# A graph and expert network on one core: counting sums spread over all eight groups, expert zero's first tile started earlier, and low parts placed ahead of two neighbours

## The chip, the core and the metric

The kernel runs on one core of a Trainium2 chip. The metric is the device time of one launch in microseconds. TensorE (PE) does the matrix products, VectorE (DVE) and ScalarE (ACT) the element work, GpSimd (POOL) index work and indirect transfers, SyncE (SP) issues most of the transfers.

## What is computed

3125 rows of 256 numbers pass four residual blocks; the graph has 50000 edges in both directions and a loop at each node (103125 entries, sorted by target). Cut to what matters:

```
def conv(h, Wl, bl, Wr):                       # mean over a node's neighbours
    agg = segment_sum(h[src], dst); mean = agg / max(count, 1)
    return mean @ Wl.T + bl + h @ Wr.T
def gnn(h, ...):  return conv(relu(conv(h, W1...)), W2...)

x = x + gnn(layernorm(x), L0_gnn)              # first network
n = layernorm(x)                               # 8 experts, top 2, without gate weights
x = x + sum over the two best e of (gelu(n @ W1[e] + b1[e]) @ W2[e] + b2[e])
x = x + gnn(layernorm(x), L1_gnn)              # second network, same graph
n = layernorm(x)                               # 4 small experts, top 2, and a shared one
x = x + shared(n) + gated(n)
```

## The kernel before, in words

The rows are padded to 25 tiles of 128. A convolution's sum over neighbours is a dense product with the adjacency matrix of counts, which stays in on-chip memory as f16 (`adj`); the rows are split into a high and a low f16 part (`parts`). Every engine has a program of its own, written out in order and tied to the others by semaphores. The stages follow one another:

1. `first_block` (0 to 80 us): layer norm, the first dense products, the edge keys. `Normalise.vector_norm` (line 295) computes mean and root for a chunk of five tiles (CT) and scales them with `norm_apply` (187); after one semaphore `transpose_chunk` (203 to 207) turns them on PE. `sync` stores the products `zt` (lines 662 to 681).
2. `build_counts` (80 to 320 us, from line 1056): 88 groups of windows of the sorted edges, in 11 bodies (BODIES) of 8 groups (UNROLL). For a group DVE makes two one-hot selections (563), PE multiplies them in 12 matmuls (`count`, 1261), and ACT copies the counts into `adj` (1208). There are two slots (SLOT): DVE can select for group g when PE has counted g-2. PE then adds up the neighbours of the 288 targets of the body before (`add_up`, 1272; 100 matmuls over 25 tiles into two banks), and ACT empties the banks (`take_sums`, 1191) into memory. The 25 tiles are shared out over the groups: four or five behind each of the counts 1 to 6 of a body, none behind 7 and 0. The first body only counts. A rare case (a window with more edges than fit) has a program of its own behind `flag`, which each engine reads before the first body.
3. `second_conv` of the first network (320 to 560 us): a ring of neighbour sums is loaded and scaled on DVE (`neighbours`, 1383 and 1385), rectified on ACT (`relu`, 1388), multiplied by the two weights on PE (1925), and the product split into its high part on ACT (`high`, 1865) and its low part on DVE (`take`, 1713). As parts come, PE sums early output tiles (1949), later ones in `one_tile` (1964). At its end come layer norm and gate, a rank and a place for each row and choice (`choose`, `put`), in seven groups of tiles of SIZES (4, 4, 4, 4, 4, 3, 2), and POOL scatters the rows to their experts' slots (`slots_in`, CAP rows for each expert). `Route` (2078 to 2158) then builds tables with the tile count, first tile and slot address; SP and ACT clear the 256 slots behind each expert's last row (`clear`, 2109 to 2121, four transfers each, and the tail of `x1`).
4. `experts` (582 to 812 us, 2162 to 2340): 28 tiles of 256 rows (ST) over the 8 experts. SP loads a tile (2205), PE turns it (2230), ACT copies it, PE does the first product (2237), ACT gelu (2292), PE the second product (2247), which is issued behind the turn of the next tile. DVE adds the bias into the one output buffer `y` (2306) when the adds of the tile before have landed, POOL copies the ids (2323) and issues two indirect transfers that add the rows to `x1` (2328).
5. `weigh_and_sum` (812 to 1013 us): layer norm of the second network in chunks, its first convolution over the finished `adj`.
6. `second_conv` again, for the second network (1013 to 1232 us, without routing), and `last_experts` (to 1382 us).

The change touches `count` and `add_up`'s order on PE and what answers it on DVE and ACT, the order in front of `take(0)` in `second_conv`, `Route`, `experts`, `Normalise`, and `first_block`'s stores.

## Time and profile before

| | us |
|---|---|
| median of 3 runs | 1375.41 (1374.94 to 1382.29) |
| the profiled execution | 1383.73 |
| its span | 1382.3 |
| PE busy | 1233.4 (89%) |
| PE weight load busy | 919.0 (66%) |
| DVE busy | 576.0 (42%) |
| ACT busy | 400.6 (29%) |
| POOL busy | 163.8 (12%) |

The profile is of one execution, whose time is 8.3 us above the median; durations in the trace are from that one. Its page gives each engine's busy time and the busy share in 40 slices; the table of stretches gives the same for stretches of one's own choice, with the clock granted to PE (1.00 is 2.4 GHz, 0.50 is 1.2 GHz). In the timeline a row is a run of like instructions: start, length, engine, line, what is written from what, how many, and in square brackets the engine's idle time just before and what ended it. `PEld` is the load of weights beside PE, `SPq` the queue of SP, where transfers are issued.

### The profile page before, as it was taken

How to read it: one execution, taken by the hardware profiler on the slowest of the kernel's cores; microseconds unless marked ns; L12 is line 12 of the kernel's file. 1: busy time of each engine (PE TensorE's matmuls, PEld its weight loads, DVE VectorE, ACT ScalarE, POOL GpSimd, SP SyncE). 2: the span in 40 equal slices, each digit the busy share in tenths (PEclk: the TensorE clock that was granted, in tenths of full speed). 3: DMA queues.
4: the chain of work that ended last, by engine and by line, in shares of the span. 5: the costliest groups of instructions: out<-in, count | busy, mean ns of one | idle time of the engine just before them, and what ended most of it. 6: DMA issues, size and time to landing. Idle time of an engine off the chain costs nothing. (4 is left out here: it accounts for less than half of the span.)

```text
span 1382.3 us, 22037 instructions
## 1 busy us (share of the span) xinstructions
PE 1233.4 (89%) x7906; PEld 919.0 (66%) x7906; DVE 576.0 (42%) x1495; ACT 400.6 (29%) x798; POOL 163.8 (12%) x177
## 2 busy tenths in 40 slices
PE   5969999998999987199999949999979999989998
PEld 4648778775668665088888837655546677866675
DVE  7857777753445545300101026200024444256444
ACT  3543443431221001164446513300012211123322
POOL 4000000000000424334344410000000000000000
PEclk9989999999999989599999979999999999989999
DMA  6200000015652323535664542120046533135001
GB/s 195 74 22 10 17 11 15 17 32 132 174 137 85 100 81 96 174 57 102 138 130 76 99 93 83 57 64 28 27 101 166 152 125 120 65 91 169 19 19 36
DMA packets 133067, 117.03 MB, mean 85 GB/s; under 512 B 22691, under 2 KB 121380, under 8 KB 132993
## 3 DMA queue, kind: packets, MB, share of 16 engines
q1 hardware_dynamic: 100896, 74.71, 19.0%
q0 software_dynamic: 11984, 18.77, 7.1%
q10 hardware_dynamic: 20112, 22.56, 4.9%
q8 instruction: 48, 0.79, 0.3%
q14 instruction: 27, 0.21, 0.1%
HBM read 67.01 MB, written 48.99 MB: 84 GB/s over the span
## 5 line engine op out<-in xcount | busy, mean ns | idle before, releaser
L1272 PE MATMUL b_pa<-adj,l_parts 128*128 (+1 forms) x1100 | 145.6, 287 | 1.9 <-ACT ring L1191 1.9
L1208 ACT ACTIVATE adj<-b_pw 128x450 f32 (+1 forms) x176 | 87.1, 550 | 136.9 <-PE b_pw L1261 136.9
L1272 PEld LDWEIGHTS b_pa<-adj,l_parts 128*128 128x128 f16 x1100 | 106.1, 98 | 26.7 <-ACT adj L1208 2.0
L563 DVE TENSOR_TENSOR ring<-it,key 128x1800 f16<-128x1800 f16 x88 | 96.3, 1094 | 55.6 <-PE b_pw L1261 54.3
L1261 PE MATMUL b_pw<-ring,room 128*128 128x150 f16 x1056 | 86.7, 234 | 25.4 <-DVE room L563 18.4
L2306 DVE TENSOR_TENSOR ring<-l_sum,l_parts 128x512 f32<-128x512 f32 x28 | 19.4, 692 | 215.0 <-DMA x<-ring,l_ids_now 114.8
L2247 PE MATMUL l_sum<-l_parts,ring 128*128 128x256 f32 x448 | 104.2, 385 | 4.1 <-ACT ring L2292 0.6
L1964 PE MATMUL l_sum<-l_parts,adj 128*128 128x256 f16 x750 | 95.0, 286 | 10.6 <-issue 10.6
L1261 PEld LDWEIGHTS b_pw<-ring,room 128*128 128x128 f16 x1056 | 76.8, 100 | 32.0 <-DVE room L563 22.0
L2247 PEld LDWEIGHTS l_sum<-l_parts,ring 128*128 128x128 f32 x448 | 82.8, 190 | 21.0 <-ACT ring L2292 10.9
L1964 PEld LDWEIGHTS l_sum<-l_parts,adj 128*128 128x128 f16 x750 | 75.0, 102 | 30.8 <-issue 19.5
L2328 POOL DMA_INDIRECT x<-ring,l_ids_now x56 | 86.6, 1546 | 56.2 <-DVE ring L2306 47.6
L1383 DVE SCALAR_TENSOR_TENSOR ring<-ring,unscale 128x256 f32<-128x256 f32 x50 | 23.9, 477 | 160.0 <-DMA ring<-inv 160.0
L1964 PE MATMUL l1b_sum<-l_parts,adj 128*128 128x256 f16 x750 | 84.8, 273 | 0.0
L563 DVE TENSOR_TENSOR room<-ib,low 128x1536 f16<-128x1536 f16 x88 | 83.7, 951 | 0.0
L1964 PEld LDWEIGHTS l1b_sum<-l_parts,adj 128*128 128x128 f16 x750 | 72.6, 98 | 12.6 <-issue 4.3
L2530 ACT ACTIVATE l_parts<-m_bank,adj 128x320 f32<-128x320 f32 x90 | 47.0, 528 | 80.2 <-PE m_bank L2477 53.6
L1949 PEld LDWEIGHTS l1b_sum<-l_parts,adj 128*128 128x128 f16 x500 | 49.8, 100 | 24.6 <-issue 13.1
L1949 PE MATMUL l1b_sum<-l_parts,adj 128*128 128x256 f16 x500 | 60.6, 278 | 4.7 <-DVE l_parts L1713 4.7
L1949 PEld LDWEIGHTS l_sum<-l_parts,adj 128*128 128x128 f16 x500 | 48.8, 98 | 22.1 <-issue 12.6
L1949 PE MATMUL l_sum<-l_parts,adj 128*128 128x256 f16 x500 | 58.5, 273 | 2.8 <-DVE l_parts L1713 2.8
L503 PE MATMUL n_agg<-adj,l_parts 128*128 128x448 f16 (+1 forms) x300 | 60.6, 361 | 0.0
(364 smaller groups left out, 1767.0 us busy)
## 6 DMA issues: line engine op xcount, KB each, us to landing
ring<-sums_and_zt SPq DMA_DIRECT2D x50, 256.0 KB, 3.1
l_parts<-in_L_ffn_W SPq DMA_DIRECT2D x16, 512.0 KB
ring<-slots_in SPq DMA_DIRECT2D x28, 257.0 KB
pre<-room ACTq DMA_DIRECT2D x34, 128.0 KB, 1.8
ring<-inv SPq DMA_DIRECT2D x50, 64.0 KB, 3.9
ring<-x SPq DMA_DIRECT2D x5, 640.0 KB, 4.8
sums_and_zt<-room ACTq DMA_DIRECT2D x5, 640.0 KB, 3.1
adj<-xt SPq DMA_DIRECT2D x5, 640.0 KB, 4.5
```

Of the source, the lines that this page charges most:

```text
L503: ins = nc.tensor.matmul(pairs[n % 3][f][:, 0:size], parts[:, k, a, f * P:(f + 1) * P], moving, start=start and a == 0, stop=stop and a == 1)
L563: return nc.vector.tensor_tensor(out.rearrange("p r (h two) -> p r h two", two=2), names[:, 0:width].rearrange("p (h two) -> p h two", two ...
L1208: ins = nc.scalar.activation(adj[:, :, ds(group * GW * W + b * BANKW * W, BANKW * W)].rearrange("p k (w j) -> p w k j", j=W), pw[u % SLOT ...
L1261: ins = nc.tensor.matmul(to, low[:, n, :], sel[:, n, :], start=i == 0, stop=i == VIS - 1)
L1272: ins = nc.tensor.matmul(pa[f][:, :], parts[:, k, a, f * P:(f + 1) * P], adj[:, k, ds(r * BW, BW)], start=k == 0 and a == 0, stop=k == TIL ...
L1383: ch.done(nc.vector.scalar_tensor_tensor(h, h, self.g["unscale"][:, 0:1], self.inv[:, r, :].unsqueeze(1).broadcast_to([P, KD, P]), ALU.mul ...
L1949: ins = nc.tensor.matmul(acc(t), adj[:, k, t * P:(t + 1) * P], parts[:, k, a, :], start=k == 0 and a == 0 and opens(t), stop=k == TILES - ...
L1964: ins = nc.tensor.matmul(acc(t), adj[:, k, t * P:(t + 1) * P], parts[:, k, a, :], start=k == 0 and a == 0 and opens(t), stop=k == TILES - ...
L2247: ins = nc.tensor.matmul(py[:, t, :], h[:, n, t * P:(t + 1) * P], w2[:, u, n, :], start=n == 0, stop=n == HB - 1)
L2306: nc.vector.tensor_tensor(y, py, b2[:, u, :].unsqueeze(1).broadcast_to([P, NT, D]), ALU.add).then_inc(s["y_done"], 1)
L2328: pool.indirect_dma_start(out=g["x1"], in_=y[:, t, :], in_offset=None, compute_op=ALU.add, out_offset=bass.IndirectOffsetOnAxis(ap=ids_now ...
L2530: nc.scalar.activation(to, b[:, 0:SUB], ACT.Relu, bias=bias).then_inc(s["act_took"], 1)
```

## The change

- **Counting.** A body's 25 tiles of sums are shared out over all eight groups (3 tiles each, 4 for one): behind each count 1 to 7 of the body, and behind count 0 of the next one. The last body is written out behind the loop, and ACT empties the banks behind the copy of the next body's first group. The first body's eight counts, with their selections and copies, stand ahead of the read of `flag` on PE, DVE and ACT.
- **Fills.** The first 256 slots of each expert and the tail of `x1` are written in `first_block`, behind the second store of `zt`, with zeros and the ids of rows that nobody reads. The transfers that cleared slots ahead of the experts go, with the steps that made ready for them.
- **Experts.** An expert's last tile is moved back so that it ends with the expert's last row; rows that the tile before already held get the ids of nobody's rows (`least`). `Route` has 26 steps for 21, for up to 40 tiles (STMAX) instead of 32. Counts up to group 4 are raised to at least 256, so that tile 0 of expert 0 is complete when the rows of groups 0 to 3 are scattered; SP loads it after those, ahead of the tables, and PE turns it and does its first product ahead of the tables too. The tile count here stays at 28. Tile buffers move from `room` to `parts`. DVE makes the ids (the larger of the row's own and `least`) in place of POOL's copy.
- **Normalise.** Each of five tiles is handed to PE by itself.
- **Second convolutions.** `take(0)` on DVE and `high(0)` on ACT stand ahead of the third neighbour instead of behind it. It holds for both.

The diff, cut to its core:

```diff
-        norm_apply(nc, ch, xr, xr, self.mv, self.rstd)
-        ch.wait()
-        dve.sem_inc(s["norm_done"], 1)
+        for t in range(CT):
+            nc.vector.tensor_scalar(xr[:, t, :], xr[:, t, :], self.mv[:, t, 0:1], self.rstd[:, t:t + 1],
+                                    ALU.subtract, ALU.mult).then_inc(s["norm_done"], 1)
...
-        pe.wait_ge(s["norm_done"], c + 1)
...
+        pe.wait_ge(ready, before + t + 1)
...
+            def fill_slots(eng):
+                eng.wait_ge(s["nobody"], 2)
+                for e in range(E0):
+                    eng.dma_start(g["slots_in"][e * CAP:e * CAP + ST, :].rearrange("(p r) d -> p (r d)", p=P),
+                                  nobody[:, :, :].rearrange("p r d -> p (r d)")).then_inc(s["filled"], 16)
+                eng.dma_start(g["x1"][ROWS:ROWS + ST, :].rearrange("(p r) d -> p r d", p=P), nobody[:, :, 0:D]
+                              ).then_inc(s["filled"], 16)
...
+                if q == 1:
+                    fill_slots(sp)
...
+            dve.sem_inc(s["sel_ready"], SLOT)
+            for u in range(SLOT, UNROLL):
+                select(0, u)
+            flag = dve.value_load(g["flag"][0:1, 0:1])
...
+                take_counts(1, 0)
+                with act.Fori(1, BODIES - 1) as body:
+                    for u in range(1, UNROLL):
                         take_counts(body, u)
+                    take_counts(body + 1, 0)
                     take_sums(body - 1)
+                for u in range(1, UNROLL):
+                    take_counts(BODIES - 1, u)
+                take_sums(BODIES - 2)
                 work.relu_first(act, s["ahead_summed"])
                 take_sums(BODIES - 1)
 
         @block.tensor
         def _(pe):
...
+            share = lambda n: range(TILES * n // UNROLL, TILES * (n + 1) // UNROLL)
...
+            for u in range(UNROLL):
+                count(0, u)
             flag = pe.value_load(g["flag"][0:1, 0:1])
...
-                for u in range(UNROLL):
-                    count(0, u)
-                with pe.Fori(1, BODIES) as body:
-                    for u in range(UNROLL):
+                count(1, 0)
+                with pe.Fori(1, BODIES - 1) as body:
+                    for u in range(1, UNROLL):
                         count(body, u)
-                        if 1 <= u < UNROLL - 1:
-                            add_up(body - 1, range(TILES * (u - 1) // (UNROLL - 2), TILES * u // (UNROLL - 2)))
+                        add_up(body - 1, share(u - 1))
+                    count(body + 1, 0)
+                    add_up(body - 1, share(UNROLL - 1))
+                for u in range(1, UNROLL):
+                    count(BODIES - 1, u)
+                    add_up(BODIES - 2, share(u - 1))
+                add_up(BODIES - 2, share(UNROLL - 1))
                 add_up(BODIES - 1, range(TILES))
...
-            for k in range(LOADED, RING - 1):
-                neighbours(k)
             for k in range(TILES):
                 take(k)
+                if k == 0:
+                    for n in range(LOADED, RING - 1):
+                        neighbours(n)
...
-            for k in range(LOADED, RING - 1):
-                relu(k)
             for k in range(TILES):
                 act.wait_ge(s["dense_done"], k + 1)
                 nc.scalar.activation(parts[:, k, 0, :], dense_bank[k % 2][:, 0:D], ACT.Identity, scale=g["scale"][:, 1:2]
                                      ).then_inc(s["high_done"], 1)
+                if k == 0:
+                    for n in range(LOADED, RING - 1):
+                        relu(n)
...
-                for e in range(2):
-                    load_expert(sp, io, weights, e, e, table.s[f"first_w_in{e}"])
-                table.clear(sp, 0, zero)
...
+        ch.done(nc.vector.tensor_tensor(self.start, self.moved, self.last, ALU.min))
+        ch.mark(nc.vector.tensor_copy(g["from"][:, :], self.start))
+        ch.done(nc.vector.tensor_tensor(self.shift, self.moved, self.start, ALU.subtract))
+        NT = ST // P
+        shape = [P, STMAX, NT]
+        ch.done(nc.vector.tensor_tensor(self.again, self.row.unsqueeze(1).broadcast_to(shape),
+                                        self.shift.unsqueeze(2).broadcast_to(shape), ALU.is_lt))
+        nc.vector.tensor_tensor(self.least, self.again, self.nobody.unsqueeze(1).broadcast_to(shape), ALU.mult
+                                ).then_inc(s["tables_ready"], 1)
...
+    def later_tiles(eng, one_tile):
+        tiles = eng.value_load(g["tiles"][0:1, 0, 0:1], min_val=1, max_val=ONE_MOST)
+        with eng.If(tiles > 1):
+            with eng.Fori(1, tiles) as j:
+                one_tile(j)
+        with eng.Else():
+            eng.nop()
...
+        load_expert(sp, io, weights, 0, 0, table.s["first_w_in0"])
+        scattered(sp, range(SETTLED))
+        load(0, 0)
+        load_expert(sp, io, weights, 1, 1, table.s["first_w_in1"])
+        sp.wait_ge(table.s["tables_ready"], 1)
+        rows_placed(sp)
+        later_tiles(sp, load_from_table)
+        for e in range(1, E0):
+            _, at = tiles_on(sp, e)
             end = sp.value_load(g["tiles"][0:1, 2, ds(e, 1)], min_val=1, max_val=STMAX)
-            with sp.If(tiles > 1):
-                with sp.Fori(at + 1, end) as j:
-                    load(j)
-            with sp.Else():
-                sp.nop()
-            if 1 <= e < E0 - 1:
+            with sp.Fori(at, end) as j:
+                load_from_table(j)
+            if e < E0 - 1:
...
+        turn(0)
+        pe.wait_ge(table.s["first_w_in0"], LOADS)
+        first_product(0, 0)
+        pe.wait_ge(table.s["tables_ready"], 1)
+        later_tiles(pe, lambda j: step(j, 0))
...
+            dve.wait_ge(s["added"], 16 * NT * j)
+            dve.wait_ge(s["ids_ready"], j + 1)
+            nc.vector.tensor_tensor(ids_now[:, :], flat(ids), flat(least), ALU.max).then_inc(s["ids_now"], 1)
+            dve.wait_ge(s["y_mm"], j + 1)
+            nc.vector.tensor_tensor(y, py, b2[:, u, :].unsqueeze(1).broadcast_to([P, NT, D]),
+                                    ALU.add).then_inc(s["y_done"], 1)
...
-            pool.wait_ge(s["added"], 16 * NT * j)
-            pool.wait_ge(s["ids_ready"], j + 1)
-            nc.gpsimd.tensor_copy(ids_now[:, :], ids[:, ds(j * NT, NT)]).then_inc(s["ids_now"], 1)
```

PE at the entry of the counting stage (behind the last product of `first_block`), before:

```order
L963 MATMUL n_few<-adj 16x1 x12
L577 UNCONDITIONAL_BRANCH
L1224 UNCONDITIONAL_BRANCH
L1226 TENSOR_LOAD flag
L1228 COMPARE_AND_BRANCH
L1230 UNCONDITIONAL_BRANCH
```

and with the change:

```order
L976 MATMUL n_few<-adj 16x1 x12
L572 UNCONDITIONAL_BRANCH
L1247 UNCONDITIONAL_BRANCH
L1260 MATMUL b_pw<-ring,room 128x150 x96
L1281 TENSOR_LOAD flag
L1282 COMPARE_AND_BRANCH
```

The 96 matmuls of the first eight counts now come ahead of the read of the flag and its branch; before, they follow the branch.

PE at the seam of two bodies, the end of the loop's body in the counting stage, before (`b_pw` are the count's banks, `b_pa` those of the sums):

```order
L1272 MATMUL b_pa<-adj,l_parts 128x288 x4
L1272 ISA
L1272 MATMUL b_pa<-adj,l_parts 128x288 x4
L1255 REGISTER_ALU
L1261 MATMUL b_pw<-ring,room 128x150 x12
L1280 REGISTER_ALU
L1280 COMPARE_AND_BRANCH
```

and with the change:

```order
L1254 ISA
L1260 MATMUL b_pw<-ring,room 128x150 x12
L1273 ISA
L1273 MATMUL b_pa<-adj,l_parts 128x288 x4
L1273 ISA
L1273 MATMUL b_pa<-adj,l_parts 128x288 x4
L1273 ISA
L1273 MATMUL b_pa<-adj,l_parts 128x288 x4
L1273 ISA
L1273 MATMUL b_pa<-adj,l_parts 128x288 x4
L1308 REGISTER_ALU
L1308 COMPARE_AND_BRANCH
```

Before, count 7 ends the loop's body and count 0 begins it, with nothing between; now the last count of a body is followed by four tiles' sums.

SP from the experts' first weights on (`in_L_ffn` are the experts' weights), before:

```order
L2074 DMA l_parts<-in_L_ffn_b 128x256
L2118 TENSOR_LOAD l_tail
L2118 ISA x2
L2119 ISA
L2119 DMA slots_in<-l_rows 128x514
```

and with the change:

```order
L2119 DMA l_parts<-in_L_ffn_b 128x256
L2253 DMA l_parts<-slots_in 128x2x257
L2119 DMA l_parts<-in_L_ffn_W 128x2x512
L2119 DMA l_parts<-in_L_ffn_W 128x4x256
L2119 DMA l_parts<-in_L_ffn_b 128x4x1
L2119 DMA l_parts<-in_L_ffn_b 128x256
L2242 TENSOR_LOAD tiles
L2242 ISA x2
L2243 COMPARE_AND_BRANCH
L2244 UNCONDITIONAL_BRANCH
L2244 ISA
L2256 TENSOR_LOAD from
```

The four clears of SP are gone, tile 0's load stands between the two experts' weights, and a branch on the tile count of expert 0 stands ahead of tile 1's.

## Rows read from the trace of the kernel before

**Rows 1.** The page: busy time of the engines, and a group of matmuls.
```profile
PE 1233.4 (89%) x7906; PEld 919.0 (66%) x7906; DVE 576.0 (42%) x1495; ACT 400.6 (29%) x798; POOL 163.8 (12%) x177
...
L1964 PE MATMUL l1b_sum<-l_parts,adj 128*128 128x256 f16 x750 | 84.8, 273 | 0.0
```

**Rows 2.** Stretches: length, busy PE, PEld, DVE, ACT, POOL; granted clock, DMA share, GB/s.
```profile
108.00:320.00 212.00, 197.28 (x2022) 168.32 (x2019) 149.43 (x156) 83.13 (x179) 0.00 (x0) 1.00 0.06 20
545.00:582.00 37.00, 4.80 (x21) 1.77 (x19) 17.27 (x90) 1.71 (x5) 17.22 (x18) 0.58 0.72 207
582.00:588.00 6.00, 3.73 (x10) 2.90 (x11) 0.00 (x0) 3.73 (x5) 0.18 (x1) 0.50 0.16 44
```

**Rows 3.** The timeline of the counting loop, PE and DVE.
```profile
143.68 1.09 DVE L563 TENSOR_TENSOR ring<-it,key 128x1800 f16<-128x1800 f16 x1 [1.29 <-PE b_pw L1261]
145.70 0.98 PE L1261 MATMUL b_pw<-ring,room 128*128 128x150 f16 x12 [1.39 <-DVE room L563]
146.52 2.12 PE L1272 MATMUL b_pa<-adj,l_parts 128*128 x16
...
287.34 0.97 PE L1261 MATMUL b_pw<-ring,room 128*128 128x150 f16 x12 [1.39 <-DVE room L563]
```

**Rows 4.** The timeline at the end of counting, ACT and PE.
```profile
306.39 0.72 ACT L1191 ACTIVATE ring<-b_pa 128x288 f32<-128x288 f32 x2
...
307.25 12.41 PE L1272 MATMUL b_pa<-adj,l_parts 128*128 128x288 f16 x100 [1.87 <-ACT ring L1191]
```

**Rows 5.** The timeline at the entry of the counting stage, POOL and PE.
```profile
81.70 0.15 POOL L1096 MEMSET ring<- 128x64 f32 x1 [44.38 <-POOLq L577]
...
86.61 3.16 PE L1261 MATMUL b_pw<-ring,room 128*128 128x150 f16 x24 [6.99 <-issue]
...
105.06 3.11 PE L1272 MATMUL b_pa<-adj,l_parts 128*128 x16
```

**Rows 6.** The timeline ahead of and in the first expert tile.
```profile
564.87 7.97 SPq L2119 DMA_DIRECT2D slots_in<-l_rows  x4
...
571.59 0.19 DVE L2156 SCALAR_TENSOR_TENSOR from<-room 128x32 int32<-128x32 f32 x1
...
579.43 6.52 SPq L2205 DMA_DIRECT2D ring<-slots_in  x2
...
582.12 1.11 PE L2230 MATMUL l_dense<-ident,ring 128*128 128x128 f32 x4 [22.96 <-DMA ring<-slots_in]
...
591.10 3.72 PE L2247 MATMUL l_sum<-l_parts,ring 128*128 128x256 f32 x16
```

**Rows 7.** SP's waits from 540 to 620 us: line, releaser, us, how many, longest.
```profile
SPq L2193 <- DMA slots_in<-l_rows: 4.2, 1, 4.2
```

**Rows 8.** DVE's output step, line 2306: its waits (us, how many), two in the timeline.
```profile
  DMA x<-ring,l_ids_now: 114.8, 16
...
759.46 0.69 DVE L2306 TENSOR_TENSOR ring<-l_sum,l_parts 128x512 f32<-128x512 f32 x1 [6.52 <-DMA x<-ring,l_ids_now]
...
782.28 0.69 DVE L2306 TENSOR_TENSOR ring<-l_sum,l_parts 128x512 f32<-128x512 f32 x1 [7.05 <-PE l_sum L2247]
```

**Rows 9.** The timeline at the start of `weigh_and_sum`, DVE and PE.
```profile
822.01 1.71 DVE L187 TENSOR_SCALAR ring<-ring,n_mv,n_rstd 128x256 f32<-128x256 f32 x5
...
823.84 2.40 PE L207 MATMUL n_ps<-ident,ring 128*128 128x128 f32 x10 [18.38 <-DVEq L306]
```

**Rows 10.** The timeline where the two second convolutions start, DVE and PE.
```profile
335.88 0.48 DVE L1383 SCALAR_TENSOR_TENSOR ring<-ring,unscale 128x256 f32<-128x256 f32 x1 [2.67 <-DMA ring<-inv]
...
338.21 2.36 PE L1949 MATMUL l_sum<-l_parts,adj 128*128 128x256 f16 x20
...
1024.41 4.41 PE L1949 MATMUL l1b_sum<-l_parts,adj 128*128 128x256 f16 x20 [4.66 <-DVE l_parts L1713]
1029.58 0.48 DVE L1383 SCALAR_TENSOR_TENSOR ring<-ring,unscale 128x256 f32<-128x256 f32 x1 [2.31 <-DMA ring<-inv]
...
1034.28 2.35 PE L1949 MATMUL l1b_sum<-l_parts,adj 128*128 128x256 f16 x20
```

More of the change, by code:

```diff
@@ L1571, in second_conv, with scattered @@
         tile_of = lambda ap, k: ap[k * P:(k + 1) * P, :]
+        def scattered(eng, groups):
+            for c in groups:
+                eng.wait_ge(s[f"scattered{c}"], 16 * 2 * SIZES[c])
         def rows_placed(eng):
-            for c in range(FINISHES):
-                eng.wait_ge(s[f"scattered{c}"], 16 * 2 * SIZES[c])
+            scattered(eng, range(FINISHES))
             eng.wait_ge(s["x_out"], 16 * FINISHES)
-            for u in range(2):
-                eng.wait_ge(table.s[f"cleared{u}"], 16 * E0 // 2)
-            eng.wait_ge(table.s["dump_out"], 16)
         if routing:
-            follow = experts(nc, io, g, pr, parts, weights, ring, [*dense_bank, extra, *sum_bank], table, rows_placed)
+            follow = experts(nc, io, g, pr, parts, weights, ring, [*dense_bank, extra, *sum_bank], table, scattered, rows_placed)
         @block.sync
@@ L2152, in vector @@
[L2152 to L2157 removed]
+        ch.done(nc.vector.tensor_copy(g["tiles"][:, 2, :], cnt[:, 2, :]))
@@ new lines, in vector @@
+        ch.done(nc.vector.tensor_tensor(past, tables(cnt[:, 2, :]), steps(self.step), ALU.is_le))
+        ch.done(nc.vector.tensor_tensor(each, past, tables(cnt[:, 5, :]), ALU.mult))
+        ch.mark(nc.vector.reduce_sum(self.moved, each, AX.X))
+        ch.done(nc.vector.tensor_tensor(past, past, tables(cnt[:, 6, :]), ALU.mult))
+        ch.done(nc.vector.reduce_sum(self.last, past, AX.X))
+        ch.mark(nc.vector.tensor_scalar(self.last, self.last, cnt[:, 4, 0:1], None, ALU.add))
+        ch.done(nc.vector.scalar_tensor_tensor(self.moved, self.step, float(ST), self.moved, ALU.mult, ALU.add))
@@ L2158, in vector, with experts @@
         dve.wait_ge(s["tables_ready"], 1)
-def experts(nc, io, g, pr, parts, weights, space, banks, table, rows_placed):
+def experts(nc, io, g, pr, parts, weights, space, banks, table, scattered, rows_placed):
     NT = ST // P
     w1, w2, b1, b2 = weights
-    used = [0]
-    def take(*shape):
-        n = math.prod(shape)
-        at, used[0] = used[0], used[0] + n
-        names = "abcd"[:len(shape)]
-        return space[:, at:at + n].rearrange(f"p ({' '.join(names)}) -> p {' '.join(names)}", **dict(zip(names, shape)))
-    xt, h, y, xr = take(KD, ST), take(HB, ST), take(NT, D), take(NT, DW)
-    ids = ids_place(parts)
+    own = expert_space(parts)
+    xt, y, xr, ids, least = (own[n] for n in ("xt", "y", "xr", "ids", "least"))
+    h = space[:, 0:HB * ST].rearrange("p (n r) -> p n r", n=HB)
+    assert HB * ST <= MOST * DW
@@ L2223, in tensor @@
     def tensor(pe):
-        pe.wait_ge(table.s["tables_ready"], 1)
         def turn(j):
@@ L2311, in vector @@
         dve.sem_inc(s["y_done"], 1)
-        with dve.Fori(0, E0 // 2) as k:
+        one_tile(0, 0)
+        later_tiles(dve, lambda j: one_tile(j, 0))
+        tiles, at = tiles_on(dve, 0)
+        dve.wait_ge(s["y_done"], at + tiles + 1)
+        dve.sem_inc(s["w_free0"], 1)
+        expert(1, 1)
+        with dve.Fori(1, E0 // 2) as k:
             expert(k * 2, 0)
```

300 lines of the change are left out of this document (145 added, 155 removed).

## The prediction

> **What bounds the kernel now.** I read the page first: PE is busy for 1233.4 us of a span of 1382.3, DVE for 576.0 and ACT for 400.6 [rows 1], and the chain that ended last is matmuls to nine tenths. So time can be won only where PE stands idle or runs at the lower clock. The table of stretches shows where: the counting stage is 93% busy (197.28 of 212.00 us), and between the last routing step and the first expert tile PE does 4.80 us of work in 37.00, at a granted clock of 0.58 [rows 2]. Then I read the timeline around each edit, for PE's idle time and what ended it. About 0.5% of the time, 6.9 us, is what a measurement of this kernel can tell from no change. The sum is made against the profiled execution (1383.73 us, span 1382.3); the median of the runs is 1375.41, 8.3 us less, and I carry the difference in microseconds over to it.
>
> **Counting: even sums.** In each body PE counts groups 7 and 0 back to back, and then waits 1.39 us for DVE's selection, which starts at 143.68, when a count has freed its slot, and lets PE go on at 145.70, 2.0 us later [rows 3]. There are nine of these waits, the second ended at 145.70, the last at 287.34, so a body lasts (287.34 - 145.70) / 7 = 20.23 us. Without the wait it is 8 counts at 0.81 us from start to start (145.70 to 146.52) and 100 sums in 12.25 (12.41 at the stage's end [rows 4], less the last one's lap over what follows): 18.7 us. With sums after every count, count g can start 1.47 + 0.81 + 1.47 = 3.7 us after count g-2 ended, more than the 2.0 that DVE needs: the wait goes. **A new one comes**: one count (0.8 us) now stands between a body's last sums and the next body's first, which need the banks emptied. ACT takes 0.72 us for both banks and PE follows 0.14 after it [rows 4]; with as much ahead of ACT that is 1.0, so 0.2 us of waiting per body. A body becomes 18.9 us: 9 x 1.33 = **12.0 us**. At the stage's end PE waits 1.87 us for ACT [rows 4], which empties the last count ahead of the sums; in the new order the count is long done and 0.9 is left: **1.0 us**. The twelve microseconds of sums that close the stage stay. Ends: 9 (each body waits 0.5 for ACT) and 14.
>
> **Counting: the first body ahead of the branch.** PE's first count starts at 86.61 after 6.99 us of idle time, though POOL works at 81.70 [rows 5]. From about 82.0 on, 4.6 us could be won. But the branch is only moved behind count 7, PE's stall with it. DVE and ACT pass theirs with less code, so DVE prepares two groups meanwhile, and of the 5 us PE gets 2 to 3 back; against that PE idles in mid-stage and may work longer at the half clock, where sixteen sums take 3.11 us [rows 5] for 2.12 [rows 3]. I take **1 us**, with -3 and 4.6 as ends. The Trainium skill (Runtime: NRT & Kernel Launch, Instruction fetch mechanics) has it that a taken branch to code outside the part already fetched waits for that fetch. By this rule the stall travels with the branch and the term is no more than 1; the row alone also allows the entry into a stage as the cause, and 4.6.
>
> **Into the experts.** Today the clears are issued until 572.84 (SP's four of the eight from 564.87), after the last scatter, the table's last step is at 571.59, SP loads rows at 579.43, PE turns them at 582.12 and reaches its first second product at 591.10 [rows 6]. SP waits 4.2 us for the clears [rows 7]; its three register reads fill the remaining 2.4. The change takes the clears out and does load, turn and first product of tile 0 inside the gap, from rows of groups 0 to 3, which are scattered while the sums still run. Then the table ends last. It has 26 steps for 21, five of them on 320 elements or more for three on 256: 1.5 us longer, 573.3. SP reads two registers (1.6) and takes a branch (0.4), loads tile 1 at 575.3; it arrives 2.7 later, is turned in 0.6, and the first second product starts at 578.6 instead of 591.10: 12.5 us. The clock is granted at 0.50 until 588 [rows 2], so the early work is cold; a step of 7 us done half at that clock loses 2.5. **10 us** remain. Ends: if the load comes no earlier than today and a whole product is cold, 591.10 - 582.7 - 3.4 = 5; if the table comes at 570 and the clock stays up, 14.
>
> **Ids by DVE.** In the expert loop the one output buffer makes a ring: the adds land, DVE writes y, POOL issues two adds. Sixteen of the 28 tiles are released by it [rows 8]; there it turns in 6.52 + 0.69 = 7.2 us at best, against PE's 7.05 + 0.69 = 7.74 per tile. DVE now does one small step (0.2 us, as the table's last [rows 6]) ahead of y, while POOL's copy, which goes, ran beside y. 0.1 us on sixteen tiles: minus **1.5 us**, between 0 and -3.5.
>
> **Normalise.** DVE scales five tiles (822.01 to 823.72), and only then PE turns them, for 2.40 us from 823.84 [rows 9]. Tile by tile PE starts near 822.5 and is bound by its own 2.4: **1.2 us**, once, since at the other chunks PE has work. Ends 0 and 1.8.
>
> **Low parts ahead of the third sums.** PE waits 4.66 us after its two dense products, until 1024.41, as ACT and DVE serve the third neighbour before the first low part. This wait goes. But the third group of sums needs a low part that is queued behind the fifth neighbour on both engines, and that one's data come at 1029.58, by SP's own issues. In the first layer they come at 335.88 and these sums start at 338.21, 2.3 later [rows 10]. So here they start at 1031.9 for 1034.28: **2.4 us**, and in the first layer, where they already wait for it, **0**. Ends for both together: 0 and 7.
>
> **Early fills.** Nine writes of 256 KB go behind the second zt store, in the first stage. SP has only stores left there, and the gathers that POOL issues meanwhile are small. I cost them at nothing; without that cover, 2.3 MB at the 207 GB/s of the gap [rows 2] are 11 us. The reordered memset and iota of POOL run ahead of its wait for DVE.
>
> **Sum**: 12.0 + 1.0 + 1 + 10 - 1.5 + 1.2 + 2.4 = 26.1 us. The profiled time would be 1357.6, the median 1349.
>
> **Rivals.** (a) **Branches cost more.** Each new one stalls its engine with nothing beside it: the counting one in full (-3 for 1) and expert 0's on SP and PE (5 of the 10). For it: 6.99 us at the entry. Against: the last layer has a branch in each of 15 tiles, and PE's idle time before these 750 matmuls is 0.0 [rows 1]. 9 us less: 1358. (b) **The gap yields more.** The table's steps stood idle for some 5 us, which the clears' traffic may have caused, and tile 0's work may keep the clock up: 3 of table, 2.5 of clock, 3 of entry, 1341. (c) **The other side.** The ring of adds becomes the bound: it nearly is. From 1.2 us per tile beyond the present slack on, 28 tiles eat the 26.1 us and 6.9 more; at 1.3 each the kernel takes 1385. It would need DVE's new step, with its two waits, to cost ten times what its size costs. (d) **The even sums gain nothing**, because the first sums wait for ACT as long as the count waited for DVE: 12 less, 1361. Against it is ACT's 0.72 us.
>
> **Chances.** Forecast 0.6, (a) 0.15, (b) 0.12, (d) 0.06, (c) 0.03, and 0.04 for (a) and (d) together, at 1370. The range of 1338 to 1363 takes in all but the last two and the ends of the forecast's terms that don't fall together. Faster by over 0.5% (below 1368.5) 0.93, same 0.04, slower 0.03.
>
> **What would show it.** A body's pitch of 18.9 us, with a wait of some 0.2 named ACT; PE's first count near 82 and a hole of 4 to 5 us behind the eighth; tile 1's load 30.5 us after SP's first weight load (34.6 is where tile 0's stands now), the first second product 34 us after it; 7.74 to 7.85 us per tile; in the last layer no wait before the first sums, but one before the third. I am wrong if the pitch stays above 20, if tile 1's load comes later than today's first, or if a tile takes 8 us.

## The result, and the profile after

The change takes 1368.61 us in the median (15 runs, 1363.35 to 1373.98) where the kernel before takes 1379.66 beside it (15 runs, 1371.88 to 1386.86): the ratio is 0.9921, with a 95% interval of 0.9898 to 0.9944. That is 11 us gained (8 to 14); 26 were forecast, and 1368.6 lies above the range of 1338 to 1363. The profiled executions lie 12.8 us apart in span (1382.3 and 1369.5).

The kernels of the experiments were measured in five groups, each against the kernel before in the same rounds. That kernel took 1364.1, 1361.4, 1364.5, 1387.5 and 1363.9 us in them, so one chip is not like another, and only ratios are compared. In its second measurement the change came to 0.9870 (0.9836 to 0.9905).

The page of the change, parts 1 and 5 (against [rows 1]):

```profile
PE 1243.6 (91%) x7906; PEld 927.3 (68%) x7906; DVE 581.7 (42%) x1531; ACT 360.3 (26%) x765; POOL 159.6 (12%) x151
...
L1273 PE MATMUL b_pa<-adj,l_parts 128*128 (+1 forms) x1100 | 148.4, 287 | 2.5 <-ACT ring L1209 2.5
...
L2361 DVE TENSOR_TENSOR l_ids_now<-l_parts 128x2 int32 (+1 forms) x28 | 4.5, 161 | 209.5 <-DMA x<-l_parts,l_ids_now 198.9
```

ACT does 40 us less. In the expert loop of before it loaded a function table 34 times, which the forecast did not look at; 33 of these loads are gone (experiment e4 below asks what that did). The last row is the one to look at: DVE's new step waits 198.9 us for adds to land. Before, the adds released DVE's output in sixteen tiles for 114.8 us [rows 8], now in 26.

The timeline of the change at the entry of counting and at two seams of bodies, PE (against [rows 3 to 5]):

```profile
80.14 1.74 PE L976 MATMUL n_few<-adj 128*128 128x1 f16 x60
83.66 3.16 PE L1260 MATMUL b_pw<-ring,room 128*128 128x150 f16 x24 [1.78 <-PEq L572]
...
101.08 2.80 PE L1260 MATMUL b_pw<-ring,room 128*128 128x150 f16 x24 [3.35 <-DVE room L558]
103.67 2.27 PE L1273 MATMUL b_pa<-adj,l_parts 128*128 x12
...
123.31 1.64 PE L1273 MATMUL b_pa<-adj,l_parts 128*128 x12 [0.18 <-ACT ring L1209]
...
142.33 1.64 PE L1273 MATMUL b_pa<-adj,l_parts 128*128 x12 [0.17 <-ACT ring L1209]
...
293.54 12.41 PE L1273 MATMUL b_pa<-adj,l_parts 128*128 128x288 f16 x100 [0.89 <-ACT ring L1209]
```

A body lasts 142.33 - 123.31 = 19.02 us (20.23 before), and in place of DVE's 1.39 us stands a wait of 0.18 for ACT. The hole at the entry is 1.78 us for 6.99, and one of 3.35 has come behind the eighth count, where the flag is now read. (Its row names DVE, but DVE had the ninth group's selection done at 98.57, 2.5 us before PE starts on it; the other 0.9 us are what PE waits for DVE at each of the counts before.)

PE from the last rank to the second product of the first tile (against [rows 6]; L2281 turns, L2288 is the first product, L2298 the second):

```profile
544.76 0.19 PE L2037 MATMUL l_sum<-l_mask,l_tri 128*128 128x16 f16 x1 [3.72 <-issue]
...
544.83 1.09 PE L2281 MATMUL l_dense<-ident,l_parts 128*128 128x128 f32 x4
...
561.05 1.12 PE L2281 MATMUL l_dense<-ident,l_parts 128*128 128x128 f32 x4 [7.93 <-DMA l_parts<-slots_in]
561.96 5.50 PE L2298 MATMUL l_sum<-l_parts,ring 128*128 128x256 f32 x16
567.29 1.03 PE L2288 MATMUL l_dense<-l_parts 128*128 128x256 f32 x4
```

Before, the last rank was at 558.94 and this second product at 591.10 [rows 6], 32.2 us later; now it is 17.2. It takes 5.50 us for 3.72, at a granted clock of 0.69 between 562 and 568 us, so 13.2 of the 15.0 us are kept. At its end (567.5 for 594.8) the change is 27 us ahead, all that was forecast for the whole kernel.

Then it loses. DVE in the expert loop of the change:

```profile
567.49 0.69 DVE L2363 TENSOR_TENSOR l_parts<-l_sum,l_parts 128x512 f32<-128x512 f32 x1 [10.66 <-PE l_sum L2298]
575.56 0.16 DVE L2361 TENSOR_TENSOR l_ids_now<-l_parts 128x2 int32 x1 [7.37 <-DMA x<-l_parts,l_ids_now]
575.63 0.68 DVE L2363 TENSOR_TENSOR l_parts<-l_sum,l_parts 128x512 f32<-128x512 f32 x1
584.01 0.16 DVE L2361 TENSOR_TENSOR l_ids_now<-l_parts 128x2 int32 x1 [7.69 <-DMA x<-l_parts,l_ids_now]
...
607.70 0.69 DVE L2363 TENSOR_TENSOR l_parts<-l_sum,l_parts 128x512 f32<-128x512 f32 x1
618.72 0.16 DVE L2361 TENSOR_TENSOR l_ids_now<-l_parts 128x2 int32 x1 [10.34 <-ACT l_parts L2334]
...
797.35 0.69 DVE L2363 TENSOR_TENSOR l_parts<-l_sum,l_parts 128x512 f32<-128x512 f32 x1
```

From the first output to the last it takes 797.35 - 567.49 = 229.9 us, 8.51 per tile; before it took 210.6, 7.80 per tile. The loop gives back 19.2 us. The shortest distance of two outputs is 7.45 us for 7.12, and six distances of 8.9 to 12.1 stand out, one for each expert's weights that SP loads meanwhile. (The row at 618.72 names ACT, whose copy of that tile's ids was long done; ids and output wait for the adds there too.)

The starts of `weigh_and_sum` and of both second convolutions (against [rows 9, 10]):

```profile
813.42 1.70 DVE L300 TENSOR_SCALAR ring<-ring,n_mv,n_rstd 128x256 f32<-128x256 f32 x5
...
813.89 2.39 PE L200 MATMUL n_ps<-ident,ring 128*128 128x128 f32 x10 [18.85 <-DVE ring L300]
...
308.45 5.37 PE L1959 MATMUL l_dense<-room,ring 128*128 128x512 f32 x8 [2.50 <-ACTq L1894]
...
323.72 2.36 PE L1983 MATMUL l_sum<-l_parts,adj 128*128 128x256 f16 x20 [1.38 <-DVE l_parts L1742]
...
1005.61 5.37 PE L1959 MATMUL l1b_dense<-room,ring 128*128 128x512 f32 x8 [3.00 <-issue]
...
1021.48 2.36 PE L1983 MATMUL l1b_sum<-l_parts,adj 128*128 128x256 f16 x20 [2.00 <-DVE l_parts L1742]
```

PE starts 0.47 us behind the first scaled tile, for 1.83. The third sums stand 15.9 us behind the dense products in the second network, and 15.3 in the first.

### The profile page after: what moved, and what is told of

It is laid out like the page before. It is cut to its first block and busy times, and to the rows that moved or that the text cites. A ratio compares the mean times of both kernels' runs of the same rounds, so it can differ in the third digit from the quotient of the medians.

```text
span 1369.5 us, 21893 instructions
## 1 busy us (share of the span) xinstructions
PE 1243.6 (91%) x7906; PEld 927.3 (68%) x7906; DVE 581.7 (42%) x1531; ACT 360.3 (26%) x765; POOL 159.6 (12%) x151
## 5 line engine op out<-in xcount | busy, mean ns | idle before, releaser
L1273 PE MATMUL b_pa<-adj,l_parts 128*128 (+1 forms) x1100 | 148.4, 287 | 2.5 <-ACT ring L1209 2.5
L2298 PE MATMUL l_sum<-l_parts,ring 128*128 128x256 f32 x448 | 111.4, 405 | 14.0 <-DVE l_parts L2363 10.8
L2298 PEld LDWEIGHTS l_sum<-l_parts,ring 128*128 128x128 f32 x448 | 88.3, 202 | 32.5 <-issue 11.4
L2394 POOL DMA_INDIRECT x<-l_parts,l_ids_now x56 | 87.3, 1559 | 160.7 <-DVE l_parts L2363 152.1
L2361 DVE TENSOR_TENSOR l_ids_now<-l_parts 128x2 int32 (+1 forms) x28 | 4.5, 161 | 209.5 <-DMA x<-l_parts,l_ids_now 198.9
L1260 PEld LDWEIGHTS b_pw<-ring,room 128*128 128x128 f16 x1056 | 77.8, 100 | 15.3 <-DVE room L558 9.6
L1742 DVE SCALAR_TENSOR_TENSOR l_parts<-l1b_dense,scale,l_parts 128x256 f16<-128x256 f32 x25 | 12.1, 484 | 138.8 <-ACT l_parts L1897 138.7
L1983 PEld LDWEIGHTS l_sum<-l_parts,adj 128*128 128x128 f16 x500 | 48.8, 98 | 21.4 <-issue 12.8
```

The lines of the kernel that those rows point to most:

```text
L1260: ins = nc.tensor.matmul(to, low[:, n, :], sel[:, n, :], start=i == 0, stop=i == VIS - 1)
L1273: ins = nc.tensor.matmul(pa[f][:, :], parts[:, k, a, f * P:(f + 1) * P], adj[:, k, ds(r * BW, BW)], start=k == 0 and a == 0, stop=k == TIL ...
L1983: ins = nc.tensor.matmul(acc(t), adj[:, k, t * P:(t + 1) * P], parts[:, k, a, :], start=k == 0 and a == 0 and opens(t), stop=k == TILES - ...
L2298: ins = nc.tensor.matmul(py[:, t, :], h[:, n, t * P:(t + 1) * P], w2[:, u, n, :], start=n == 0, stop=n == HB - 1)
L2394: pool.indirect_dma_start(out=g["x1"], in_=y[:, t, :], in_offset=None, compute_op=ALU.add, out_offset=bass.IndirectOffsetOnAxis(ap=ids_now ...
```

## The experiments

Each diff is against the change unless said otherwise. "Mean" is the time from the first expert output to the last, over 27, in the profiled execution.

**What lengthened the expert loop.** Two theories stood: A, SP's loads of rows now come earlier (1.6 us behind PE's turn for 2.9) and run into the adds; B, the ring of adds is longer by itself. In e1 DVE raises `rows_free` behind its wait for the adds.

```diff
+            if behind:
+                sp.wait_ge(s["rows_free"], j)
             sp.dma_start(xr, ...)
```

> The changed kernel, but SP loads the rows of an expert tile only when the adds of two tiles before have landed (a semaphore that DVE raises when it passes its wait for them), so the 257 KB load no longer runs beside the adds. Theory A (collision: the loads are issued 1.6 us behind PE's turn where they were issued 2.9 us behind it before, and run into the adds' traffic): the six tiles of expert 0 come at 7.7 us instead of 8.1, the experts' stage loses 8 to 16 us, the kernel takes 1353 to 1361 for 1368.6. Theory B (the ring of adds is longer by itself, since DVE makes the ids and waits twice inside it): no change, 1366 to 1371, or 1 to 2 us slower, since loads only come later.

```diff
-            dve.wait_ge(s["added"], 16 * NT * j)
             dve.wait_ge(s["ids_ready"], j + 1)
-            nc.vector.tensor_tensor(ids_now[:, :], flat(ids), flat(least), ALU.max).then_inc(s["ids_now"], 1)
+            nc.vector.tensor_tensor(flat(ids), flat(ids), flat(least), ALU.max).then_inc(s["ids_max"], 1)
+            dve.wait_ge(s["added"], 16 * NT * j)
...
         def add_rows(j):
+            pool.wait_ge(s["added"], 16 * NT * j)
+            pool.wait_ge(s["ids_max"], j + 1)
+            nc.gpsimd.tensor_copy(ids_now[:, :], flat(ids)).then_inc(s["ids_now"], 1)
```

> The changed kernel, but DVE takes the larger id ahead of its wait for the adds, in place, and POOL copies the ids beside y, as in the kernel before; same output. Theory A: the shortest distance of two outputs goes back from 7.5 to 7.2 us, but tiles whose loads run beside the adds stay at 8 and more; 2 to 7 us gained (1362 to 1367). Theory B: the experts' stage goes back to what it was (7.8 us per tile for 8.5), 15 to 19 us gained (1350 to 1354).

Both together:

> Both edits. Theory A: expert 0 at 7.74 and faster recovery behind each load of weights, 12 to 20 us gained (1349 to 1357), a few more than with the load held alone. Theory B: the same as with the ids on POOL alone.

Against the kernel before, one line ahead of ACT's expert loop:

```diff
+        nc.scalar.activation(warm[0:1, :], g["scale"][0:1, 0:1], ACT.Gelu)
```

> The kernel before, with one gelu on a single number ahead of the expert loop of ACT, which should take the 34 table loads of 1.28 us out of the tiles of experts 0, 2, 4 and 6 and let SP load their rows 1.3 us earlier. Theory A: ACT does 43 us less, and yet the kernel gets slower by 5 to 15 us (1385 to 1395 against 1379.7), expert 0's outputs no longer at 7.74 but at 7.8 to 8.3. Theory B: no change within 2 us, or slightly faster.

| | ratio to before | 95% interval | mean, us |
|---|---|---|---|
| e1, rows held | 0.9828 | 0.9800 to 0.9857 | 8.17 |
| e2, ids on POOL | 0.9754 | 0.9725 to 0.9783 | 7.74 |
| e3, both | 0.9778 | 0.9751 to 0.9804 | 7.96 |
| e4, before with one table | 0.9986 | 0.9967 to 1.0004 | 7.83 |

The page's rows for e4, ACT, and for e2, DVE (from the groups by line):

```profile
L2296 ACT ACT_TABLE_LOAD x1 | 1.3, 1283 | 15.8 <-issue 15.8
```

```profile
L2363 DVE TENSOR_TENSOR l_parts<-l_sum,l_parts 128x512 f32<-128x512 f32 x28 | 19.4, 692 | 181.0 <-PE l_sum L2298 105.8 <-DMA x<-l_parts,l_ids_now 75.2
```

e2 is the finding: DVE waits for PE again in most of its idle time, a tile takes PE's 7.74 us, and the kernel is the quickest of all. e4 goes against A by itself: one of the 34 table loads is left, SP loads rows as early as in the change, and nothing gets slower; expert 0's outputs stay at 7.74. But A's sign came in e1: expert 0's first five distances, 7.6 to 8.4 us in the change, are 7.7 to 7.8 with the rows held. So the early rows cost something where the ring is longer, and nothing where it is not. Over the whole kernel, holding them helps the change a little (0.9828 against 0.9870 as it was measured later, intervals that overlap) and does nothing for e2. So B is right in kind. But a ring of 7.5 us does not explain 8.5, and B's 15 to 19 us do not follow from its own length.

**The change again, the ids step in the old kernel, and two other terms.**

> The changed kernel itself, unaltered, so that it is measured on the same chip and in the same rounds as the others. Every theory: about 0.992 of the kernel before, as measured.

Against the kernel before (DVE's loop runs from `at` to `end` there, as in the change):

```diff
                 dve.wait_ge(s["added"], 16 * NT * j)
+                dve.wait_ge(s["ids_ready"], j + 1)
+                nc.vector.tensor_copy(ids_now[:, :], ids[:, ds(j * NT, NT)]).then_inc(s["ids_now"], 1)
...
-            pool.wait_ge(s["added"], 16 * NT * j)
-            pool.wait_ge(s["ids_ready"], j + 1)
-            nc.gpsimd.tensor_copy(ids_now[:, :], ids[:, ds(j * NT, NT)]).then_inc(s["ids_now"], 1)
```

> The kernel before, with this one part of the change: DVE makes the ids between the landing of the adds and the output, in place of POOL's copy beside it. Theory B (0.3 to 0.4 us more inside the ring tip it over PE's 7.74 us per tile, and a late output then meets the next load of rows and weights at a worse place): outputs at 7.5 us at best, 8.3 to 8.6 on average for 7.8, kernel 12 to 22 us slower than before. The prediction's pricing (a small step costs its own length on the tiles that the ring releases): 1.5 to 4 us slower.

Against e2, from here to e12. The loops of PE and ACT as before (`add_up` behind counts 1 to 6, `take_sums` behind each body):

> The changed kernel with the ids on POOL (the quickest so far, 0.975 of the kernel before), and with the sums shared out as before, over counts 1 to 6. If the even sums gain what the prediction says, it is 13 us slower than that kernel (0.985 of the kernel before) and a body takes 20.2 us instead of 19.0; if PE's idle time there was covered elsewhere, less than 6.

```diff
-        load(0, 0)
         load_expert(sp, io, weights, 1, 1, table.s["first_w_in1"])
         sp.wait_ge(table.s["tables_ready"], 1)
         rows_placed(sp)
+        load(0, 0)
```

> The changed kernel with the ids on POOL, and with the load of expert 0's first tile issued only behind the tables and the last scatter, as before; the clears stay out. If the early tile is what gains in the gap, 7 to 10 us slower than with the ids on POOL alone (0.981); if the clears' traffic was what held the tables and the load, less than 4.

| | ratio to before | 95% interval | mean, us |
|---|---|---|---|
| e5, the change | 0.9870 | 0.9836 to 0.9905 | 8.45 |
| e6, before with DVE's ids | 1.0050 | 1.0030 to 1.0070 | 8.10 |
| e7, old sums | 0.9836 | 0.9805 to 0.9867 | 7.76 |
| e8, tile 0 late | 0.9783 | 0.9752 to 0.9814 | 7.74 |

e6 costs 7 us, between the two expectations: more than the prediction's price, less than B's. Its rows come as late as before, and expert 0's outputs stay at 7.74, which fits what e1 says of the change. e7 gives back 0.8% (e2 0.9754), some 11 us, and its waits of 1.39 us are back: the even sums gain what was forecast. e8's profile tells the two parts of the gap apart. PE in e4 (before's experts, with the clears) and in e8 (no clears, tile 0 late), and the second product of e2:

```profile
534.96 0.20 PE L2003 MATMUL l_sum<-l_mask,l_tri 128*128 128x16 f16 x1 [3.71 <-DVE l_mask L1791]
...
566.07 3.72 PE L2248 MATMUL l_sum<-l_parts,ring 128*128 128x256 f32 x16
```

```profile
522.30 0.19 PE L2037 MATMUL l_sum<-l_mask,l_tri 128*128 128x16 f16 x1 [3.72 <-DVE l_mask L1820]
...
546.09 3.72 PE L2298 MATMUL l_sum<-l_parts,ring 128*128 128x256 f32 x16
```

```profile
520.27 0.20 PE L2037 MATMUL l_sum<-l_mask,l_tri 128*128 128x16 f16 x1 [3.71 <-DVE l_mask L1820]
...
538.18 5.42 PE L2298 MATMUL l_sum<-l_parts,ring 128*128 128x256 f32 x16
```

From the last rank to the second product it is 31.1 us with the clears, 23.8 without, and 17.9 with the early tile, whose cold product gives 1.7 back. Without the clears it is 7.3 us less, although the tables take 1.8 us longer, and the early tile is worth 4.2. In the rounds e8 loses 4 us against e2, with intervals that overlap.

**A step of the same size with no use, and three more terms.**

```diff
             dve.wait_ge(s["added"], 16 * NT * j)
+            nc.vector.tensor_copy(pad[:, 0:NT], row_f).then_inc(s["pad"], 1)
+            dve.wait_ge(s["pad"], j + 1)
```

> The changed kernel with the ids on POOL, and one more small step of DVE with a wait (some 0.35 us together) between the landing of the adds and the output. It makes nothing that is used. If it is the length inside the ring that tips it, the outputs fall back to 7.5 us at best and 8.2 to 8.5 on average, and the kernel loses 10 to 18 us (1340 to 1347 on this chip) for 28 x 0.35 = 10 us at most of added steps, of which a ring with slack would show none. If it was something else in the change's way of making ids (the address from a register, the wait for the ids), 0 to 4 us slower.

The read of the flag ahead of the first body on PE, DVE and ACT:

> The changed kernel with the ids on POOL, and the flag read and its branch taken ahead of the first body, as before (the first body's code stands in both arms). By the profile of the change PE's first sums come 3.6 us earlier relative to the stage before, so 3 to 4 us slower; by the prediction's term 1 us slower; if the half clock eats what the order gives, no difference.

Without the call of `fill_slots`:

> The changed kernel with the ids on POOL, without the nine early writes. It leaves out the filling of the first 256 slots of each expert and of the tail of x1, of which nothing is read with these inputs. If the writes cost the 1 to 2 us by which the first stage ends later in the profile of the change, 1 to 2 us faster; if that came from the clock or from the steps around them, no change.

`neighbours(n)` and `relu(n)` of the third neighbour ahead of `take(0)` and `high(0)`:

> The changed kernel with the ids on POOL, with the third neighbour and its relu ahead of the first low and high parts again, in both second convolutions. By the prediction 2.4 us slower, all of it in the second network; by the profile of the change 3.1 (2.3 there and 0.8 in the first network).

| | ratio to before | 95% interval | mean, us |
|---|---|---|---|
| e9, idle ring step | 0.9790 | 0.9761 to 0.9819 | 8.08 |
| e10, branch first | 0.9787 | 0.9758 to 0.9815 | 7.87 |
| e11, no fills | 0.9755 | 0.9724 to 0.9785 | 7.74 |
| e12, neighbours back | 0.9787 | 0.9750 to 0.9824 | 7.74 |

e9 makes the shortest distance 7.28 us for e2's 7.09, half of what the ids added, and the mean 8.08 for 7.74. It is a miss: its median is 6 us above that of the quickest kernel of its group (e11), where 10 to 18 were expected if the length decides and 0 to 4 if it does not. The intervals of e9, e11 and e2 overlap, and e2's own kernel has a mean of up to 8.00 in other profiles (below). So e9 leans to the length, but that a step without use costs as much as the ids did is not shown. e10's profile has the old entry back; its 24 first counts start here:

```profile
83.62 3.18 PE L1266 MATMUL b_pw<-ring,room 128*128 128x150 f16 x24 [6.80 <-issue]
```

From the end of the stage before (matmuls at 75.10) to its first sums at 102.04 it is 26.9 us, and 23.2 in e2 (76.35 to 99.53): 3.8 us (2.8 to 3.7 against the other three of its group). e11 shows no gain in the rounds. e12's third sums are 1.9 and 1.7 us later than e2's behind the dense products, and its rounds (0.9787 for 0.9754, overlapping) agree without proving it.

**Why so much more than the step's length.** Two kernels without the weights of experts 2 to 7 (these compute with those of experts 0 and 1), and e2 beside them:

```diff
-                load_expert(sp, io, weights, e + 1, u, s[f"w_in{u}"])
```

> The change itself (ids made by DVE inside the ring), without the loads of weights for experts 2 to 7, which compute with the weights of experts 0 and 1; it leaves out 6 MB of transfers. If the excess over 7.74 us per tile comes through the weights' transfers that meet the adds, the seven distances of 9 to 12 us go, the mean falls from 8.45 to 7.8 to 8.0 and the kernel gains 12 to 18 us against the change (0.974 to 0.978 of the kernel before). If the ring's own length and the row loads make it, the mean stays above 8.2 and it gains 3 to 6 us.

> The same weights left out of the kernel with ids on POOL. Its ring has slack, and the weights cost it little: mean 7.74 or less, 0 to 2 us faster than e15.

> The kernel with the ids on POOL once more, in the same rounds. 0.975 of the kernel before, as measured.

| | ratio to before | 95% interval | mean, us |
|---|---|---|---|
| e13, change, two weights | 0.9797 | 0.9764 to 0.9830 | 7.87 |
| e14, e2, two weights | 0.9742 | 0.9710 to 0.9773 | 7.74 |
| e15, e2 again | 0.9797 | 0.9758 to 0.9835 | 8.00 |

In e13 the ring is as long as in the change (7.56 us at best), and yet the mean is 7.87: of the six long distances none is left, and the longest is 8.61. The excess comes with the weights' transfers, 27 x (8.51 - 7.87) = 17 us of it in the profiles; in the rounds e13 is 0.7 to 1.2% below the change's two measurements, 10 to 17 us. Expert 0's first five distances stay at 7.7 to 8.5, with the rows as early as in the change. e14 is a miss: 0 to 2 us under e15 were expected, and it is 7 (intervals that just overlap). e15's loop came to 8.00 and not to 7.74, so the weights cost this kernel too, where its outputs fall late. In the change and in the kernel before, SP issued them so (SP's queue in the change, then in before; the outputs ahead of them are at 607.70 and 633.56):

```profile
611.65 0.92 SPq L2119 DMA_DIRECT2D l_parts<-in_L_ffn_W  x2
```

```profile
639.16 1.97 SPq L2074 DMA_DIRECT2D l_parts<-in_L_ffn_W  x2
```

The two adds of a tile are issued 1.5 and 3.4 us behind its output, and the second lands 7.0 us behind it at the earliest (median 7.2 before, 7.6 in the change). The 1 MB of weights came 5.6 us behind the output before, and the next output was 8.51 us away; in the change it came 3.95 behind, beside the second add, and the next was 11.10 away. Over before, e2 and the two profiles of the change, weights issued 2.4 to 4.0 us behind an output gave 10.3 to 12.1 us (eight times), 4.8 to 6.9 behind it 7.7 to 8.5 (seven times; one at 4.4 gave 9.66), and 0.8 to 1.0 behind it 8.1 to 10.0 (eight times). All 18 profiles that load the weights say the same: issued 2.1 to 4.4 us behind an output they gave 9.5 to 12.1 us (28 times), at 4.6 or later 7.6 to 8.7 (32 times); the four in between gave 8.4 to 9.6, and those within 1 us of the output 8.1 to 10.8.

That the bytes alone do it does not fit what e2's own kernel shows. At its eleventh output e15 and e2 issue the same weights; DVE, SP and DVE in e15, then in e2:

```profile
644.12 0.69 DVE L2363 TENSOR_TENSOR l_parts<-l_sum,l_parts 128x512 f32<-128x512 f32 x1 [7.01 <-DMA x<-l_parts,l_ids_now]
...
647.66 0.89 SPq L2119 DMA_DIRECT2D l_parts<-in_L_ffn_W  x2
...
655.30 0.69 DVE L2363 TENSOR_TENSOR l_parts<-l_sum,l_parts 128x512 f32<-128x512 f32 x1 [7.62 <-DMA x<-l_parts,l_ids_now]
```

```profile
621.49 0.69 DVE L2363 TENSOR_TENSOR l_parts<-l_sum,l_parts 128x512 f32<-128x512 f32 x1 [6.31 <-DMA x<-l_parts,l_ids_now]
...
626.48 0.98 SPq L2119 DMA_DIRECT2D l_parts<-in_L_ffn_W  x2
...
629.46 0.69 DVE L2363 TENSOR_TENSOR l_parts<-l_sum,l_parts 128x512 f32<-128x512 f32 x1 [4.41 <-DMA x<-l_parts,l_ids_now]
```

3.54 us behind the output they gave 11.18 us, 4.99 behind it 7.97. The two profiles are of different chips, but e18's alone has both as well: 5.39 gave 7.75 and 3.02 gave 10.59.

**Can the moment be moved?** A count of issued adds, raised by POOL behind the second add, that SP waits for ahead of the weights:

```diff
+                sp.wait_ge(s["issued"], end + 1)
                 load_expert(sp, io, weights, e + 1, u, s[f"w_in{u}"])
```

> The change with all its work, but SP issues an expert's 1 MB of weights only when POOL has issued both adds of the tile in flight, some 5 us behind its output instead of 2.5 to 4. If the moment decides, the distances of 10 to 12 us go down to 8 to 9, the mean from 8.45 or 8.5 to 8.0 to 8.2, and the kernel gains 6 to 12 us against the change (0.980 to 0.985 of the kernel before). If the bytes alone decide, the mean stays above 8.35 and the gain is below 3 us.

> The same hold in the kernel with the ids on POOL. Its outputs are at 7.74 to 8.0 on average already; where a run fell behind (e15: 9.5 to 11.2 at four weights' loads) this should go: 0 to 5 us faster than e18, and a narrower spread.

> The kernel with the ids on POOL, unaltered, in the same rounds: 0.975 to 0.98 of the kernel before.

| | ratio to before | 95% interval | mean, us |
|---|---|---|---|
| e16, change, weights held | 0.9868 | 0.9840 to 0.9895 | 8.40 |
| e17, e2, weights held | 0.9783 | 0.9755 to 0.9812 | 7.86 |
| e18, e2 once more | 0.9766 | 0.9738 to 0.9795 | 7.95 |

e2's kernel itself comes to 7.74, 8.00 and 7.95 in three profiles, so it too falls behind in some runs, and e17 is no better than chance beside it. e16 is a miss: its mean of 8.40 is what was expected if the bytes alone decide. But it tests neither, for the moment did not move: in e16's profile SP issued the weights 3.09 us behind the sixth output, ahead of the second add's issue at 3.41, and 2.5 to 2.8 behind three others, so the hold did not do what it was to do. That the moment decides rests on the pattern of the profiles above; no run sets it and shows it by itself.

## Why the prediction was wrong, point by point

**Ids by DVE** is the step that failed: "DVE now does one small step (0.2 us ...) ahead of y ... 0.1 us on sixteen tiles: minus 1.5 us, between 0 and -3.5". Measured, the loop lost 19.2 us in the profiles, and putting the ids on POOL gave 1.0 to 1.2% of the kernel, 14 to 17 us (e2 and e18 against e5; e15 against the first measurement). Three errors lie on top of each other. The step was priced by its 0.16 us beside y; but its address comes from a register, and that register work stands inside the ring too. DVE's step of the change, by line:

```profile
L2361 DVE TENSOR_TENSOR l_ids_now<-l_parts x28: 160/161/163, 556.7 to 797.3; 128x2 int32 x27, 128x2 int32<-128x2 int32 x1
L2361 DVEq FUSED_REGOPS  x27: 93/99/110, 575.3 to 797.1; - x27
L2361 DVEq ALU_OP  x27: 40/40/45, 575.5 to 797.2; - x27
```

So the ring grew by 0.3 us (7.45 for 7.12). It was applied to the sixteen tiles that the ring released, not to a ring of 7.45 us that has 0.29 us left under PE's 7.74, where 7.12 had 0.62: a delay is made up half as fast. And the large term was missing: an output that is late moves against SP's transfers of rows and weights, which follow PE, and then waits for adds that run beside them (about 17 of the 19 us go with the weights, e13). One of the prediction's own signs of being wrong came, "if a tile takes 8 us": it takes 8.51. Rival (c) named this ring, priced it from 1.2 us per tile on and gave it 0.03; it came at 0.71, enough to eat more than half of the gain, not to turn its sign. Its condition, "ten times what its size costs", was the wrong test: most of the cost came with the collisions and not with the step's length.

**Even sums**: forecast 12.0 + 1.0, body 18.9 us, wait for ACT 0.2. Measured: body 19.02, wait 0.18, the last wait 0.89 for 1.87; from the first sums to the last hundred it takes 189.9 us for 202.2, 12.3 us in all. Right. Rival (d) is out.

**The first body**: forecast 1 (-3 to 4.6). From the last matmuls of the stage before to the first sums it takes 23.5 us for 27.2, 3.6 us, and e10 shows 3.8. The size was wrong, inside its ends. The stall did not travel whole: 6.99 us became 1.78 at the entry and 3.35 behind the branch, 2.5 of them not DVE's, and DVE worked through it. By the rule of the Trainium skill (Runtime: NRT & Kernel Launch, Instruction fetch mechanics), that a taken branch waits for the fetch of code outside the part already fetched, I had let the whole stall go with the branch. The trace agrees with it only in part, by these 2.5 us; whether they are the fetch or the read of the flag no run tells. Rival (a), half of it on this branch, is out.

**Into the experts**: forecast 10 (5 to 14), measured 13.2. The table was 26 steps and longer, as said (from the last rank to its end 8.8 us in e2, 7.0 in e4; in the profiles of the change and of before 11.7 and 12.8, with DVE idle between the steps). I gave most of the credit to the early tile; on e4, e8 and e2 the clears were 7.3 of it and the tile 4.2. The cold product, 1.7 us, was counted as 2.5. Rival (b), a gap that yields more, holds by 3 us of its 8, but not for its reasons: the clock did not stay up, and the idle time in the table was not the clears' doing, for e4 has the clears and not the idle time. What it was stays open.

**Normalise**: forecast 1.2, measured 1.83 - 0.47 = 1.4. **Low parts**: forecast 2.4 in the second network, measured 18.2 - 15.9 = 2.3; in the first 0.8 where 0 was said.

**Early fills**: nothing was costed. The first stage ends at 80.14 for 77.90, 2.2 us later; between 40 and 44 us, from ahead of the first fill (41.28) on, the granted clock was 0.52 and 0.62, where it was 1.00 before. e11, without the fills, ends the stage 1.4 us sooner than e2, but is those 1.4 us ahead already at the store before the fills (37.29 for 38.65), and from there both take 37.70 us. So the fills cost nothing there, as costed; where the 2.2 come from stays open.

The terms as measured are 12.3 + 3.6 + 13.2 - 19.2 + 1.4 + 3.1 - 2.2 = 12.2, and the spans differ by 12.8. But for the even sums, 0.7 us short, the first stage and the ids, the forecast's terms were met or surpassed. That the sum meets the spans to 0.6 us is in part luck, since each term is read to some tenths only. Without the ids step in the ring the change gains some 30 us: e2 does (0.9754 to 0.9797, 28 to 34 us). e2 is the quickest version that computes everything; it beats both kernels.

## What to carry to other kernels

Where a ring of waits (a landing, a step, an issue, a transfer) is only a few tenths shorter than the bound's period, price a step put into it not by its length alone but by what a late ring does: which transfers keep the bound engine's time, and where they meet the ring's own when it slips. Take into account the waits and the address work that come with the step, and put whatever does not need the landed data ahead of the wait. Look for the shortest and the longest periods in the trace, and not only at the mean: here the shortest told the ring's length and the longest told the collision.

## What the runs showed of the hardware that was not expected

- Where one expert's weights (two transfers of 512 KB) were issued beside a tile's second indirect add, the distance of two outputs was 10.3 to 12.1 us for 7.5 at best; issued 5 us behind the output they cost 0 to 0.8.
- One gelu of one number ahead of a loop took 33 table loads of 1.28 us out of it (e4: one load where the kernel before has 34), and the time did not move, since ACT was not waited for.
- The kernel before differed by 2% between groups of runs. In its slower profile and in that of the change PE's sums of the first network (750 matmuls) show 10.6 and 9.2 us of idle time that nothing in the trace explains; in e13 and e15, taken where the kernel before ran at 1387, there are 11.2 and 10.8, and in e2, where it ran at 1364, 0.0. What it is was not tried.
